# State-space stage: B and C rows broadcast from two float32r parts where three bf16 parts were, TensorE's steps without loops

## What is computed

```python
xz = x @ W_in.T                      # 512 channels xp, 512 channels z
xc = silu(conv_b + causal 4-tap convolution of xp)
dbc = xc @ W_x.T                     # 128 columns dt, 16 columns Bm, 16 columns Cm
delta = softplus(dt @ W_dt.T + b_dt)
dA  = exp(delta[..., None] * A)      # A = -exp(A_log), 16 states per channel
dBx = delta[..., None] * Bm[:, :, None, :] * xc[..., None]
h_t = dA_t * h_(t-1) + dBx_t         # over 512 tokens
y   = sum over states of h * Cm + xc * Dp
out = (y * silu(z)) @ W_out.T
```

## Time and profile before

| | us |
|---|---|
| median of 3 runs | 981.3 |
| lowest and highest | 980.85 and 983.6 |
| the profiled execution | 979.24 |
| its span, from first to last instruction | 977.4 |
| TensorE, VectorE, ScalarE, GpSimd busy | 783.4, 617.0, 408.4, 280.4 |

### The profile page before, as it was taken

One profiled execution on the slowest core, in us unless ns is written; L12 is line 12 of the kernel. 1 busy time (PEld: TensorE's weight loads), 2 busy tenths in 40 slices (PEclk: granted clock), 3 DMA queues, 4 the chain that ended last, 5 costly groups with the idle time before them and its releaser, 6 DMA issues.

```text
span 977.4 us, 12528 instructions
## 1 busy us (share of the span) xinstructions
PE 783.4 (80%) x3915; PEld 525.1 (54%) x3915; DVE 617.0 (63%) x899; ACT 408.4 (42%) x623; POOL 280.4 (29%) x240
## 2 busy tenths in 40 slices
PE   4999946757892766799998999964886478899997
PEld 3688812223450222268886777742454245577776
DVE  5544579999869998964545655465514551564544
ACT  3563556545364553523442233260375037232321
POOL 0000046756406675620059700000000001990000
PEclk9999976989995897999999999986798689999999
DMA  9000000000000000024000000043002300000000
GB/s 313 25 2 1 1 0 0 0 0 1 0 0 0 0 0 0 0 64 136 0 1 0 1 1 0 0 99 103 15 1 74 109 15 0 0 1 1 22 1 21
DMA packets 21231, 24.67 MB, mean 25 GB/s; under 512 B 2746, under 2 KB 18821, under 8 KB 21157
## 3 DMA queue, kind: packets, MB, share of 16 engines
q1 hardware_dynamic: 19942, 23.57, 8.2%
q10 hardware_dynamic: 1254, 0.66, 0.3%
HBM read 19.92 MB, written 4.29 MB: 25 GB/s over the span
## 4 chain that ended last, share of the span: by engine, by line
PE 54%; DVE 21%; issue 10%; DMA 6%; ACT 4%; SPq 3%; POOL 1%; DVEq 1%; POOLq 0%; ACTq 0%
PE PS L379 37%; DVE shared L1263 6%; DVE shared L1273 6%; DMA scratch_k<-shared 3%; PE PS L562 2%; SPq L1517 2%; DMA shared<-scratch_q 2%; PE PS L702 2%; ACT shared L989 2%; POOL shared L1558 1%; PE PS L602 1%; PE PS L522 1%; PE PS L477 1%; PE PS L389 1%; PE PS L652 1%
## 5 line engine op out<-in xcount | busy, mean ns | idle before, releaser
L379 PE MATMUL PS<-xnT,weights_r 128*128 (+2 forms) x1176 | 291.6, 399 | 1.6 <-DVE xnT L1103 1.6
L379 PEld LDWEIGHTS PS<-xnT,weights_r 128*128 128x128 f32 (+1 forms) x1176 | 214.5, 187 | 53.1 <-issue 4.8
L1558 POOL TENSOR_TENSOR shared<-shared,xn_tok 128x1024 f32<-128x1024 f32 x64 | 150.4, 2351 | 85.5 <-DVE shared L1273 77.1
L1120 DVE TENSOR_TENSOR gated<-gated,PS 128x512 f32<-128x512 f32 (+1 forms) x84 | 57.7, 687 | 166.9 <-ACT gated L804 166.3
L1571 POOL TENSOR_TENSOR weights_r<-moe_raw,cols 128x256 fp32r<-128x256 f32 (+2 forms) x78 | 51.4, 672 | 346.5 <-PE PS L702 270.6
L804 ACT ACTIVATE gated<-PS 128x512 f32<-128x512 f32 (+1 forms) x84 | 50.3, 598 | 233.9 <-PE PS L379 212.4
L1273 DVE TENSOR_TENSOR_SCAN shared<-PS,shared 128x1024 f32<-128x1024 f32 x64 | 145.9, 2282 | 0.0
L379 PE MATMUL PS<-weights_r,work_r 128*128 128x256 f32 x800 | 141.2, 293 | 2.9 <-DVE work_r L1127 2.8
L562 PE MATMUL PS<-shared,cf 128*128 128x512 f32 x256 | 126.6, 622 | 0.0
L379 PEld LDWEIGHTS PS<-weights_r,work_r 128*128 128x128 f32 x800 | 118.0, 192 | 15.0 <-issue 11.5
L919 ACT ACTIVATE PS<-shared,cols 128x511 f32<-128x511 f32 x128 | 83.1, 682 | 29.1 <-DVE PS L1301 16.0
(11 more groups left out here) (172 smaller groups left out, 982.2 us busy)
## 6 DMA issues: line engine op xcount, KB each, us to landing
shared<-in_L_ffn_W_dram SPq DMA_DIRECT2D x3, 1024.0 KB, 11.4
moe_raw<-in_L_ffn_w_dram SPq DMA_DIRECT2D x4, 704.0 KB, 6.5
scratch_k<-shared SPq DMA_DIRECT2D x12, 128.0 KB
scratch_q<-shared SPq DMA_DIRECT2D x12, 128.0 KB
shared<-scratch_k SPq DMA_DIRECT2D x8, 192.0 KB
shared<-scratch_q SPq DMA_DIRECT2D x8, 192.0 KB
moe_raw<-in_L_ffn_w_dram SPq DMA_DIRECT2D x1, 1408.0 KB, 7.8
x_tok<-in_L_attn_x_dram SPq DMA_DIRECT2D x2, 512.0 KB, 8.2
```

Of the source, the lines that this page charges most:

```text
L379: last = nc.tensor.matmul(o, lhs[l], rhs[r], start=(start and i == 0), stop=(stop and i == 2))
L1120: return nc.vector.tensor_tensor(g, g, bank(2 + slot)[0:rows, :], ALU.mult)
L1558: nc.gpsimd.tensor_tensor(hc[:, u * 2 * T:(u + 1) * 2 * T].rearrange("p (c t) -> p c t", c=2), hst[:, (u % 2) * 2 * T:(u % 2 + 1) * 2 * T] ...
```

## The change

The rows of B and C are split into two parts where there were three. ScalarE writes the rows, rounded to float32r (a float32 format that TensorE multiplies in one pass), into both halves of a new 64-row `bc_stack`. VectorE overwrites rows 32 to 63 with the unrounded rows less the rounded ones. ScalarE's copy stands behind chunk 0 of its softplus and ahead of chunk 2. The broadcasts of B and C multiply these 64 rows by `pick_r`, a float32r copy of `pick` that VectorE makes at the start of the program. TensorE's inner loop and its loop over the batches in this stage are written out.

```diff
--- before.py
+++ after.py
@@ -199,9 +199,8 @@
 
         sp_pos = [hc[:, c * T:(c + 1) * T] for c in range(EC)]
         sp_low = [hc[:, (EC + c) * T:(EC + c + 1) * T] for c in range(EC)]
-        c_bc, bc_stack = xn_tok, combT
-        bc_rest = hst[:, 0:T]
-        bc_hi, bc_mid = hst[:, T:3 * T // 2].bitcast(BF16), hst[:, 3 * T // 2:2 * T].bitcast(BF16)
+        c_bc = xn_tok
+        bc_stack, pick_r = sb("bc_stack", T, F32R), sb("pick_r", 32, F32R)
         decay = [bank(at, 2) for at in PAIR_BANK]
 
         q_stack, a = cut(shared, 0, NH * T, BF16)
@@ -257,7 +256,7 @@
         for st in (MOE0, MOE1):
             S[st] = stage_sems(st, ("up", "silu", "prod", "high", "hid", "used", "score", "sig", "sigt",
                                     "comb", "combt", "combT", "cb", "mixed"))
-        S[MAMBA] = stage_sems(MAMBA, ("xp", "z", "ini", "tap", "xc", "zs", "dt", "dtT", "bc", "stack", "dl", "abs",
+        S[MAMBA] = stage_sems(MAMBA, ("xp", "z", "ini", "tap", "xc", "zs", "dt", "dtT", "bc", "bc_hi", "stack", "dl", "abs",
                                       "e", "ln", "u", "sp", "dx", "dx_p", "col0", "B", "C", "cev", "dA", "mul",
                                       "scan", "hc", "ys", "yf"))
 
@@ -548,13 +547,13 @@
 
                 def broadcast_b(half, n):
                     pe.wait_ge(s["mul"], HEAD + (b * 2 + half) * DS + n)
-                    nc.tensor.matmul(bank(B_BANK), pick[0:96, bass.ds(n, 1)].broadcast_to([96, P]),
-                                     bc_stack[0:96, :], start=True, stop=True).then_inc(s["B"], 1)
+                    nc.tensor.matmul(bank(B_BANK), pick_r[0:64, n:n + 1].broadcast_to([64, P]),
+                                     bc_stack[0:64, :], start=True, stop=True).then_inc(s["B"], 1)
 
                 def broadcast_c(half, n):
                     pe.wait_ge(s["cev"], HEAD + (b * 2 + half) * DS + n)
-                    nc.tensor.matmul(bank(C_BANK), pick[0:96, bass.ds(n + DS, 1)].broadcast_to([96, P]),
-                                     bc_stack[0:96, :], start=True, stop=True).then_inc(s["C"], 1)
+                    nc.tensor.matmul(bank(C_BANK), pick_r[0:64, n + DS:n + DS + 1].broadcast_to([64, P]),
+                                     bc_stack[0:64, :], start=True, stop=True).then_inc(s["C"], 1)
 
                 def add_state(half, n, slot, stop=False):
                     pe.wait_ge(s["hc"], HEAD + (b * 2 + half) * DS + n + 1)
@@ -592,7 +591,7 @@
                     if half:
                         pe.wait_ge(s["yf"], b * 3 + 1)
                         open_sums()
-                    with pe.Fori(1, DS // 4 - 1) as q:
+                    for q in range(1, DS // 4 - 1):
                         quad(q)
                     quad(DS // 4 - 1, final=True)
 
@@ -906,7 +905,10 @@
                         act.wait_ge(s["u"], b * 4 + (2 * SOFTPLUS_POOL.index(c) + 1))
                         nc.scalar.activation(low, low, ACT.Identity, bias=minus_one).then_inc(s["u"], 1)
 
-                for c in SOFTPLUS_ORDER:
+                softplus_parts(SOFTPLUS_ORDER[0])
+                act.wait_ge(s["bc"], b + 1)
+                nc.scalar.activation(bc_stack[0:64, :], bank(1)[0:64, :], ACT.Copy).then_inc(s["bc_hi"], 1)
+                for c in SOFTPLUS_ORDER[1:]:
                     softplus_parts(c)
                 act.wait_ge(s["col0"], b + 1)
                 act.wait_ge(a_ready, 2)
@@ -1035,6 +1037,8 @@
                 dve = self.dve
                 nc.vector.memset(minus_one, -1.0)
                 nc.vector.memset(cols[:, 49:50], 0.0)
+                dve.wait_ge(ld["const"], 32)
+                nc.vector.tensor_copy(pick_r[0:64, :], pick[0:64, :])
                 nc.vector.memset(ones_row[0:1, :], 1.0).then_inc(col_ready, 1)
                 dve.wait_ge(ld["x0"], 16)
                 self.norm(0, 1)
@@ -1244,15 +1248,9 @@
 
                 softplus(0)
 
-                dve.wait_ge(s["bc"], b + 1)
-                ps = bank(1)[0:96, :]
-                self.link(v.tensor_copy(bc_hi[0:96, :], ps))
-                v.tensor_copy(bc_stack[0:32, :], bc_hi[0:32, :])
-                self.link(v.tensor_tensor(bc_rest[0:96, :], ps, bc_hi[0:96, :], ALU.subtract))
-                self.link(v.tensor_copy(bc_mid[0:96, :], bc_rest[0:96, :]))
-                v.tensor_copy(bc_stack[32:64, :], bc_mid[32:64, :])
-                self.link(v.tensor_tensor(bc_rest[0:96, :], bc_rest[0:96, :], bc_mid[0:96, :], ALU.subtract))
-                v.tensor_copy(bc_stack[64:96, :], bc_rest[64:96, :]).then_inc(s["stack"], 1)
+                dve.wait_ge(s["bc_hi"], b + 1)
+                low = bc_stack[32:64, :]
+                v.tensor_tensor(low, bank(1)[32:64, :], low, ALU.subtract).then_inc(s["stack"], 1)
                 softplus(1)
                 dve.wait_ge(s["dx"], (b + 1) * 2)
 
@@ -1648,7 +1646,7 @@
             prog.prepare()
             prog.base = prog.n
             prog.stage(lambda b: prog.ffn(FFN0, b), 3, peeled=True)
-            prog.stage(prog.mamba, 19)
+            prog.stage(prog.mamba, 15)
             prog.stage(lambda b: prog.ffn(FFN1, b), 3)
             prog.stage(lambda b: prog.moe(MOE0, b), 20)
             prog.stage(prog.attention, 14)
@@ -1660,7 +1658,7 @@
             prog = TensorProgram(pe)
             prog.prepare()
             over_batches(pe, lambda b: prog.ffn(FFN0, b), peeled=True)
-            over_batches(pe, prog.mamba)
+            over_batches(pe, prog.mamba, peeled=True)
             over_batches(pe, lambda b: prog.ffn(FFN1, b))
             over_batches(pe, lambda b: prog.moe(MOE0, b))
             pe.wait_ge(ld["bo"], 16)
```

## The result

| | us |
|---|---|
| median of before, 19 runs | 981.44 |
| median of after, 19 runs | 984.16 |
| ratio | 1.0027, 95% interval 1.0016 to 1.0038 |
| the profiled execution of after, its span | 987.2, 985.4 |

The change makes the kernel slower by 0.27%, between 1.6 and 3.7 us, where I forecast 1.4 us faster. The forecast's sign and its range were wrong.

A forecast was written before the change was run, and what follows sets the result against it. The prediction took VectorE to bound the scan, and TensorE then VectorE the opening; -1.84 us for the openings and +0.4 for the broadcasts made -1.4, from 981.3 to 979.9 us, range 977.3 to 983.2.

The forecast's parts named there:

- What bounds the kernel: State-space stage: TensorE, then VectorE's own row in the opening; VectorE in the scan, held up by TensorE six times, 5.6 us.
- The opening: From the rows of B and C to the first multiplication: shorter split less ScalarE's wait and GpSimd's company, gain 0.92 us a batch.
- The turn that the prediction saw at 135.46: Chunk 1, VectorE and GpSimd ready together: gain 1.25 us if VectorE goes first, 0.2 us if GpSimd does.
- The broadcasts: Scan, float32r for bf16: 0.05 us lost for each at the six waiting places, 0.4 us in all, 0 to 1.6.
- the bound from above: Scan: the broadcasts' weight load, if not hidden behind the product ahead, costs 0.09 to 0.18 us each.
- half 0's 0.4 us to spare: Scan, half 0 at 1.2 GHz: B's broadcast ends 0.4 us before VectorE takes it, enough for three times 0.05.
- the range of the clock's rise: Scan, start of half 1: the clock's rise differs between batches, adding 0.6 us on either side of the range.
- Rival (c): Scan: a 64-row float32r broadcast costs two passes, 5.2 us lost in both batches, time 984.7 us; chance 0.09.
- (a): Opening: ScalarE's wait is free, so the split's full saving of 5.6 us a batch comes, 970.5 us; chance 0.04.
- (b): Opening: VectorE's last operation of chunk 1 escapes GpSimd, 0.95 us back a batch, time 978.0 us; chance 0.10.
- The loops and the copy at the start: TensorE's loops written out and VectorE's copy of pick before the first norm: worth nothing and nothing lost.
- The sum: Whole kernel: -1.84 us for the opening plus 0.4 for the broadcasts, -1.4 us, giving 979.9 us.

The follow-up runs named there:

- e2_bf16: The changed kernel with the two parts and the weights in bf16, 64 rows, and without the copy of pick; 980.41 against 981.77 us, ratio 0.9983.
- e3: The changed kernel with VectorE instead of ScalarE making the rounding copy, ahead of its subtraction; 978.18 us against 981.77 for before, ratio 0.9963.
- e4: The changed kernel with the copy of pick moved behind the first norm and the first weights; 984.96 us against 982.37 for before, ratio 1.0019.
- e1: The kernel before with only TensorE's inner loop and batch loop in the state-space stage written out; 982.07 against 981.77 us, ratio 1.0001.
- e6: The kernel before, three bf16 parts kept, with its split in five VectorE instructions for seven; 980.40 against 982.37 us, ratio 0.9977.
- e7: The changed kernel with float32r broadcasts over 128 rows, the added rows zero; 979.07 us against 982.37 for before, ratio 0.9964.
- e9: The changed kernel with VectorE making the rounding copy and float32r broadcasts over 128 rows; 972.55 us against 981.96 for before, ratio 0.9910.
- e10: The changed kernel with float32r broadcasts over 96 rows, the last 32 zero; one run, 976.18 us against 981.96 for before.
- e5: The changed kernel with VectorE making the rounding copy and bf16 parts and weights, 64 rows; 973.83 us against 981.77 for before, ratio 0.9904.

## Why the prediction was wrong

**What bounds the kernel** was read rightly: the differences in the state-space stage are in the openings and in VectorE's waits for the broadcast of B (3.75 of the scans' 3.94 us).

**The opening** was right in its mechanism and a little small in size. ScalarE's idle time was 2.95 us (forecast 2.9), VectorE's 3.63 (3.6), chunk 1's four operations 1.63 each, and the gain 1.28 us a batch where I took 0.92 and had 1.25 as one end. The turn that the prediction saw at 135.46, and that came at 136.04, went to VectorE in both batches: its L1245 took 0.42 us there, where the same operation took 0.71 before. In e2_bf16's batch 0 the opening took 0.25 us more than in its batch 1, but the turns are the same in both; the difference is in the idle time behind chunk 1's last operation (0.52 us for 0.29), and its cause is open. The sum of the openings is -2.56 us where I had -1.84.

**The broadcasts** are the step that failed. I had 0.4 us for them, with 1.6 us as the upper end. The scans of the float32r kernels with 64 rows (after, e3, e4) take 220.1 to 220.6 us, those of the kernels with 96 bf16 rows (before, e1, e6) 215.8 to 216.2: a loss of 4.3 us where I had 0.4. Neither half of the change costs that alone. The float32r kernels with 96 or 128 rows (e7, e9, e10) take 215.2 to 216.5, so the format alone has no more than the 0.4 us of the first waits; bf16 with 64 rows (e2, e5) takes 216.6 and 217.3, about 1 us. Three things in the step were wrong. I priced a 64-row product nearer to the pitch of 128-row products, when no row of the trace had 64 rows. I let the bound from above be the load of the broadcasts themselves (four chains a batch); but the exposed load is also that of the float32 sum behind them and of the broadcast behind the sums, so each state costs TensorE 0.59 us more at 1.2 GHz, where my bound had 0.18 us for each of four broadcasts a batch (which is 1.4 us in all, and not the 1.6 that I wrote). And I took half 0's 0.4 us to spare as enough, and the range of the clock's rise as 0.6 us: with 4.86 us a state against VectorE's 3.31, each state of half 1 for which the clock stays low costs 1.5 us where it cost 1.0, in batch 1 a third wait appeared there (1.07 us), and in its half 0 the 0.4 us to spare did not suffice (a wait of 0.23 us). The clock also stayed low for longer around the start of half 1: 10.2 or 13.7 us in the float32r kernels with 64 rows, 6.8 or 10.2 us in all those with 96 or 128 rows.

**Rival (c)** had the sign and, for the most part, the places: it put the time at 984.7 (measured 984.16). Its mechanism, two passes, is not what happened: a 64-row float32r product is followed by the next after 0.33 us at the full clock and 0.59 at the half, where the float32 sums of two passes take 0.43 and 0.85. So its number is near by luck: it had 5.2 us for the broadcasts, and 1.84 for an opening that gained 2.56. I gave it 0.09. Rivals (a) and (b) did not happen.

**The loops and the copy at the start** were worth nothing, as forecast (e1, e4).

**The sum** of what is shown is -2.56 + 4.3 = +1.7 us, at the lower end of the measured 1.6 to 3.7. Whether the 1 us between it and the median is a cost elsewhere or the spread of executions, of 5 us, stays open. For the other kernels too, the stretches of the one profile and the measured ratio lie apart, on either side (e3 and e9 are 1.5 and 1.7 us slower than their stretches say, e6 and e7 1.3 and 1.4 us faster), and behind the last multiplication of the scan the profiles vary from 562.1 to 568.7 us; e4, whose stretches are the same, measured 0.4 to 3.3 us over before.

## What to carry to other kernels

A shorter operand is not a cheaper one: price a product with a new number of rows as unknown until a row with that number is seen, and try it padded to the neighbours' size. A helper step that moves to an idle engine brings a wait into that engine's queue; ask what is queued behind it before counting what the old engine saves. Here the same step cost 3.5 us a batch on idle ScalarE and 0.68 us on busy VectorE. And of two ways to shorten work beside GpSimd, reading from PSUM helped here, and having fewer instructions that read SBUF helped little.

## What the runs showed of the hardware

Weight loads hide behind the product ahead when both products use 96 or 128 rows, and not when one uses 64 and the other 128: the sum behind a broadcast starts after 0.32 us in place of 0.24 at the full clock, and a state at 1.2 GHz takes 4.86 us with 64 float32r rows, 4.67 with 64 bf16 rows, and 4.27 with 96 or 128 rows of float32r and with 96 of bf16. I had not expected the added zeros to be faster. The Trainium skill (TensorE: Matmul & The Clock Gate, section "The mechanism") lists from traces that a load overlaps a running product only when it targets another group of rows, though the same section also names the background weight buffer as a target that lets a load go ahead. The traces here differ from the first statement: loads for the same 128 rows overlap, the next one starting at 170.75 with the product ahead of it in e7_k128, and those that change between 64 and 128 rows do not.

A float32r product that follows a wait is followed by the next after 0.34 us at the full clock and 0.59 at the half with 64, 96 and 128 rows alike, a bf16 product after 0.22 and 0.40 with 64 and 96 rows. With 64 rows of float32r the step is the same without a wait.

VectorE and GpSimd take turns on instructions with SBUF operands: a VectorE operation with two of them, 0.69 us alone, then takes 1.63. One with an operand in PSUM and one in SBUF took 0.67 us beside GpSimd (L1251 in the kernel before).
